# Two engines fetch the first batch ids of a four-layer LoRA kernel, and ACT issues the second batch's weights

## The reference, cut to what matters

```python
# x: (8, 128, 512) f32; itok_B_0_15: (8,) int32
def _L0_cond_ref(x, adapter_ids, weight):          # weight: (16, 512, 512)
    w = weight[adapter_ids]
    return jnp.einsum('bsi,boi->bso', x, w)
...
x = x + _L0_cond_ref(x, itok_B_0_15, L0_cond_weight)
x = x + _L1_cond_ref(x, itok_B_0_7, ...)   # dense 512x512 + 8 routed experts of rank 16
x = x + _L2_cond_ref(x, ..., itok_B_0_4)   # dense 512x512 + a LoRA of rank 32
x = x + _L3_cond_ref(x, ..., itok_B_2_6, 0)  # gated MLP 512-1376-512 + three LoRAs of rank 16
return x
```

## Time and profile before

| | |
|---|---|
| median of 3 runs | 298.38 us (298.31 to 298.52) |
| the profiled execution | 298.5 us, of which its span is 296.7 us |
| PE busy | 286.5 us, 97% of the span |
| DVE, ACT, POOL busy | 197.0, 143.8, 45.3 us |
| granted PE clock | 1.0 throughout |
| DMA in the first 35 us | from 4 us on the 16 DMA engines are busy 55% to 104% |

### The profile page before, as it was taken

The page is one execution under the profiler, slowest core; times in us unless marked ns, Lnnn a source line. Parts: engine busy times, 40 slices in busy tenths (PEclk is TensorE's granted clock), DMA queues, the critical chain, the costliest instruction groups (busy, mean ns, idle before and its releaser), DMA issues.

```text
span 296.7 us, 4572 instructions
## 1 busy us (share of the span) xinstructions
PE 286.5 (97%) x1624; PEld 235.8 (79%) x1624; DVE 197.0 (66%) x343; ACT 143.8 (48%) x255; POOL 45.3 (15%) x67
## 2 busy tenths in 40 slices
PE   5889999999999999999999999999999999999995
PEld 5358778888888788887788888888889888888884
DVE  1288897894656999897776776785747958342003
ACT  2378672513326279756646656566535783211000
POOL 1000000000804405243123213403000000000000
PEclk9999999999999999999999999999999999999999
DMA  5999974008504040300440520600193100022005
GB/s 165 342 393 395 343 243 108 0 0 248 178 0 101 0 145 0 121 23 0 124 159 4 167 115 16 197 3 26 48 354 126 56 0 0 0 73 71 0 2 141
DMA packets 23255, 33.29 MB, mean 112 GB/s; under 512 B 2624, under 2 KB 15424, under 8 KB 23104
## 3 DMA queue, kind: packets, MB, share of 16 engines
q1 hardware_dynamic: 22944, 32.47, 33.0%
q10 hardware_dynamic: 288, 0.52, 0.6%
HBM read 30.89 MB, written 2.10 MB: 111 GB/s over the span
## 4 chain that ended last, share of the span: by engine, by line
PE 86%; DVE 5%; DMA 4%; issue 2%; ACT 1%; SPq 1%; DVEq 0%; ACTq 0%
PE bank L1237 12%; PE bank L1238 12%; PE bank L1239 12%; PE bank L1360 10%; PE bank L1361 10%; PE bank L1362 10%; DMA w_raw<-in_w 4%; PE bank L1342 3%; PE bank L1192 2%; PE bank L1485 2%; PE bank L1221 1%; PE bank L1284 1%; PE bank L1174 1%; PE bank L1222 1%; PE bank L1223 1%
## 5 line engine op out<-in xcount | busy, mean ns | idle before, releaser
L546 ACT ACTIVATE part<-bank 128x512 f32<-128x512 f32 x44 | 26.1, 594 | 30.3 <-PE bank L1362 30.2
L1237 PE MATMUL bank<-act_hl,wd_hl 128*128 128x512 f32 (+1 forms) x99 | 36.5, 369 | 0.0
L1238 PE MATMUL bank<-act_hl,wd_hl 128*128 128x512 f32 (+1 forms) x99 | 36.3, 367 | 0.0
L1239 PE MATMUL bank<-act_hl,wd_hl 128*128 128x512 f32 (+1 forms) x99 | 36.2, 366 | 0.0
L1052 DVE TENSOR_TENSOR part<-bank,part 128x512 f32<-128x512 f32 x44 | 29.1, 682 | 6.7 <-PE bank L1342 6.6
L977 DVE SCALAR_TENSOR_TENSOR bgu_st<-bgu_st,lo_rows,bgu_raw 128x512 fp32r<-128x512 f32 x22 | 17.6, 836 | 11.6 <-ACT bgu_st L546 11.6
L803 DVE TENSOR_TENSOR w_hl<-w_raw,w_hl 128x512 fp32r<-128x512 f32 x29 | 19.0, 688 | 9.1 <-ACT w_hl L546 9.1
L546 ACT ACTIVATE act_hl<-act_f 128x512 fp32r<-128x512 f32 x22 | 13.6, 624 | 20.8 <-PE bank L1239 18.8
L803 DVE TENSOR_TENSOR act_hl<-act_f,act_hl 128x512 fp32r<-128x512 f32 x22 | 14.9, 691 | 12.9 <-ACT act_hl L546 12.8
L546 ACT ACTIVATE w_hl<-w_raw 128x512 fp32r<-128x512 f32 x29 | 17.7, 624 | 8.9 <-DMA w_raw<-in_w 8.6
L1239 PEld LDWEIGHTS bank<-act_hl,wd_hl 128*128 128x128 f32 x99 | 18.6, 188 | 3.1
(11 more groups left out here) (162 smaller groups left out, 695.1 us busy)
## 6 DMA issues: line engine op xcount, KB each, us to landing
w_raw<-in_w SPq DMA_DIRECT2D x22, 256.0 KB, 7.2
wgu_raw<-in_wgu SPq DMA_DIRECT2D x11, 512.0 KB, 4.1
bgu_raw<-in_bgu SPq DMA_DIRECT2D x40, 128.0 KB, 2.7
w_raw<-in_w SPq DMA_DIRECT2D x7, 512.0 KB, 7.6
wd_raw<-in_wd SPq DMA_DIRECT2D x4, 704.0 KB, 6.0
out<-x_f SPq DMA_DIRECT2D x7, 256.0 KB, 2.3
x_f<-in_xT SPq DMA_DIRECT2D x6, 256.0 KB, 8.4
w_raw<-in_w SPq DMA_DIRECT2D x1, 1024.0 KB, 4.9
```

Of the source, the lines that this page charges most:

```text
L546: return act.activation(dst, src, ACT.Copy)
L1237: pe.matmul(dst, w_hi, x[0][:, cols], start=start, stop=False)
L1238: pe.matmul(dst, w_hi, x[1][:, cols], start=False, stop=False)
L1239: return pe.matmul(dst, w_lo, x[0][:, cols], start=False, stop=stop)
```

## The change

SP fetches only id 0 ahead of c0 to c3. It fetches ids 2 to 7 behind c3's issue, in front of x_f of batch 2. ACT, after its two x_f transfers, fetches id 1 itself and issues the three pieces of batch 1. ids_of takes the stretch of ids and the engine as arguments, and the three issues have become the helper load_w0. The order of the waits and the buffers stay as they are.

```diff
+        def ids_of(src, last, first=0, end=B, engine=mybir.EngineType.SP):
+            _, ids = nc.values_load_multi_w_load_instructions(
+                src[0:1, first:end], engines=[engine], min_val=0, max_val=last,
...
+        W0_CUTS = ((0, 2), (2, 3), (3, 4))
+        def load_w0(queue, b, adapter):
+            for k, (first, end) in enumerate(W0_CUTS):
+                queue.dma_start(w0_raw[b % W0_RING][:, first:end],
+                                w0[adapter][:, first * D:end * D]).then_inc(w0_in[b % W0_RING][k], 16)
...
-            adapter0 = ids_of(ids0, w0.shape[0] - 1)
+            adapter0 = ids_of(ids0, w0.shape[0] - 1, 0, 1)
             for c in range(C):
                 sp.dma_start(w0_raw[0][:, c], w0[adapter0[0]][:, c * D:(c + 1) * D]).then_inc(w0c_in[c], 16)
-            for b in range(1, B):
-                adapter = adapter0[b]
-                if b >= 2:
-                    sp.dma_start(x_f[:, b], xT[b]).then_inc(x_in[b], 16)
+            adapter0 = [*adapter0, None, *ids_of(ids0, w0.shape[0] - 1, 2, B)]
+            for b in range(2, B):
+                sp.dma_start(x_f[:, b], xT[b]).then_inc(x_in[b], 16)
...
-                for k, (first, end) in enumerate(((0, 2), (2, 3), (3, 4))):
-                    sp.dma_start(w0_raw[b % W0_RING][:, first:end],
-                                 w0[adapter][:, first * D:end * D]).then_inc(w0_in[b % W0_RING][k], 16)
+                load_w0(sp, b, adapter0[b])
...
             for b in range(2):
                 act.dma_start(x_f[:, b], xT[b]).then_inc(x_in[b], 16)
+            load_w0(act, 1, ids_of(ids0, w0.shape[0] - 1, 1, 2, mybir.EngineType.Activation)[0])
```

More of the change, by code:

```diff
@@ L385, in bass_four_residual_layers @@
         block = ctx.enter_context(nc.Block())
+        def ids_of(src, last, first=0, end=B, engine=mybir.EngineType.SP):
+            _, ids = nc.values_load_multi_w_load_instructions(
+                src[0:1, first:end], engines=[engine], min_val=0, max_val=last,
+                skip_runtime_bounds_check_because="each id only forms the DRAM address of a transfer, "
+                                                  "and the transfer checks that address itself")
+            return ids
+        W0_CUTS = ((0, 2), (2, 3), (3, 4))
[3 more added lines that the diff above has]
+                                w0[adapter][:, first * D:end * D]).then_inc(w0_in[b % W0_RING][k], 16)
         @block.sync
         def _(sp):
[L390 to L396, removed]
-            adapter0 = ids_of(ids0, w0.shape[0] - 1)
+            adapter0 = ids_of(ids0, w0.shape[0] - 1, 0, 1)
             for c in range(C):
                 sp.dma_start(w0_raw[0][:, c], w0[adapter0[0]][:, c * D:(c + 1) * D]).then_inc(w0c_in[c], 16)
-            for b in range(1, B):
-                adapter = adapter0[b]
-                if b >= 2:
-                    sp.dma_start(x_f[:, b], xT[b]).then_inc(x_in[b], 16)
+            adapter0 = [*adapter0, None, *ids_of(ids0, w0.shape[0] - 1, 2, B)]
+            for b in range(2, B):
+                sp.dma_start(x_f[:, b], xT[b]).then_inc(x_in[b], 16)
                 if b == W0_RING:
```

## The result

The changed kernel is slower by 0.4%: 300.04 us in the median of 22 runs (298.81 to 302.57), beside 298.78 us for the kernel before in the same sessions (298.24 to 301.2). The ratio is 1.0039, with a 95% interval of 1.0021 to 1.0057. The forecast was 297.3 us. Three executions of those compared in this document took over 1000 us, two of the kernel before and one of e1_act_only; they are left out of the ratios.

What follows compares the result with a forecast made beforehand. Batch 3's L1221 at 21.58 us, held by the DMA queue and PE's work, sets the end. DMA side (0.4 + 0.7 = 1.1 us earlier) gives 20.5, PE side 20.4; the later gains 1.1: 297.3 us, range 296.4 to 298.5.

Steps and rivals of the forecast that it cites:

- Ids 2 to 7 behind c3: SP's second fetch, ahead of batch 2's x_f: about 2.1 us, x_f issued at 7.2, no cost while older transfers last.
- the four: The rivals: more is won (12%), single id not fetched faster (12%), batch 0 pays (22%), batch 0 pays more (10%).
- The sum: DMA side at the start: 0.4 + 0.7 = 1.1 us earlier, batch 3's first piece landing at 19.0, L1221 at 20.5.
- The PE side: c3 1.0 us later, batch 0 ending at 12.2, then 8.2 us of PE work: batch 3's L1221 at 20.4.
- the third rival: Batch 0 pays: c3 lands 1.6 to 2.2 us later, gain only 0 to 0.6, about 298.1 us; chance 22%.
- The fourth rival: Batch 0 pays more: c3 4.1 us later, batch 0 ends at 15.3, 1.9 us slower, 300.3 us; chance 10%.
- the first fetch: SP's load of id 0 alone takes 1.05 us instead of 1.48; c0 to c3 go out 0.4 us earlier.
- ACT's first issue: Batch 1's first issue, on ACT behind two register loads: at 3.8 us instead of 5.48 on SP.
- the share of 0.85 from 4 to 6.5 us: DMA share in this stretch at the start: forecast 0.7 or more, instead of 0.55; idle time filled worth 0.7 us.
- batch 1 without a wait for its weights: PE at batch 1's start: no wait before it, 0.29 us of waiting for a split gone.
- from batch 3's L1221 on everything moves along: Behind 21.58 us all hangs on PE, ACT and DVE progress, so the end shifts as much as L1221.

Runs made afterwards that it cites:

- e1_act_only: Changed kernel with SP fetching all eight ids first and no second fetch; ACT still fetches id 1 and issues batch 1: 0.9996 of the kernel before.
- e5: Changed kernel with SP's second fetch reading all eight ids from the first one on, not six from the third on: 1.0012 of the kernel before.
- e6: Changed kernel without ACT's part: SP issues batch 1 itself, and its second fetch, behind c3, reads all eight ids: 1.0024 of the kernel before.
- v8: Against the changed kernel: SP's second fetch reads eight ids behind batch 2's x_f; ACT fetches eight, issues batches 1 and 2; filler matmuls added: 0.9987 of before.
- e7_pause: Kernel before, with SP waiting for the end of batch 1's last transfer before issuing x_f of batch 2; no fetch moved: 304.24 us, one execution.
- e4: The changed kernel profiled once more, no edit, for the length of its second fetch: span 298.6 us.

## Why the prediction was wrong

*The step that failed* is the second one, "Ids 2 to 7 behind c3". It took the fetch at about 2.1 us, from the earlier trace rows, and wrote that it costs nothing, with a cover that is gone "only if the issue slips by 3 us". The fetch took 6.2 us in the profile, the issue of x_f slipped from the forecast 7.2 to 10.90, by 3.7, and the cover was gone. The bound held roughly: with the issue at 8.86 in e5 the engines stayed busy, with 10.90 they fell to a share of 0.62. The duration was wrong. The earlier trace rows held loads of one shape, eight ids from the first one, at the quiet start and at 31 and 34 us. No row had a load of another shape, or one beside the starting stream. Even for the same shape the upper end was too low: in other traces a load of eight ids at 33.7 us took 2.22 us (e6) and a pointer load at 30.4 us 2.45 (v8). That should have been an unknown price with a wide upper end, and it should have been a rival: none of the four had it.

*What the slip costs* was missing as well. I treated the queue as work at 324 GB/s or more that begins again where it stopped. In e7_pause some six microseconds at 240 to 266 GB/s follow the pause. As an estimate, six microseconds at 251 instead of 398 GB/s are a loss of 0.88 MB, 2.2 us at the full rate; in the changed kernel, 8 us at 298 are 0.80 MB, 2.0 us. The sum also left out that batch 3's first piece can't be issued before batch 0 ends: at the forecast's own 12.2 that is 1 us later than the 11.39 of before, where it counted 1.1 us earlier for its landing.

*The PE side* was mis-sized. c3 was taken 1.0 us later, with 2.1 as the upper bound. It landed at 4.3 + 7.9 = 12.2, 2.5 later, and batch 0 ended at 13.44. With the 8.2 us of PE work behind it this alone gives 21.6 for L1221 of batch 3: no gain, as the third rival had it, and the likelier course for ACT's half (e1: 0.9996). The other 0.8 us, up to 22.42, come from batch 3's late piece. The fourth rival named the right sign; in the profile of the result its cause is not the one, and its point of decision, batch 0's end at 13.4, was only just reached. In e4's execution its course came nearly to the number (batch 0's end at 15.50, it had 15.3; L1227 at 23.41, it had 23.5), but by a c1 that landed at 10.93 and a fall of the clock, which it didn't have. That its time, 300.3, is close to the measured 300.04 is luck in good part.

*Right were* the first fetch (0.83 us for one id, c0 issued at 2.65, 0.64 earlier; I had 0.4, at most 0.6; in e4 it was 0.02), ACT's first issue (3.81, I had 3.8), the share of 0.85 from 4 to 6.5 us, batch 1 without a wait for its weights, and that from batch 3's L1221 on everything moves along: 0.84 later there, 0.9 in the span. The rate in the filled stretch was 175 GB/s at that share of 0.85, though: I counted idle share as bytes won, and in a starting stream it isn't.

What stays open is why the loads take so long there. Shape and place both count, by the table. Whether an odd stretch is taken apart into several reads, and what a read waits for beside a starting stream, no run here shows. The same load of six ids took 4.41, 2.48 and 4.04 us in three executions, and nothing here says why. The Trainium skill, page "Runtime: NRT & Kernel Launch", section "Instruction fetch mechanics", gives some 200 ns for each register. At the quiet start one id took 0.58 to 0.85 us, three 1.8 and eight 1.5, which is no such line.

## What to carry to other kernels

A register load that stands between two DMA issues belongs to the transfer queue's path: price it at its worst, several microseconds beside running transfers, or put nothing urgent behind it. Keep a saturated queue from running empty: behind the pause of e7, 2.4 us of idle time from 12 to 15, the slow stretch cost about as much again by the estimate above, whatever makes it slow. A second issuing engine brought bytes forward here at the expense of the transfers beside them, so look at which of them the first consumer waits for. And take more than one trace of a kernel whose executions spread: the second one of the changed kernel lost its time in another place than the first.

## What the runs showed of the hardware

- A load of three registers from the first id on took longer than one of eight: 1.79 and 1.82 us in two traces against 1.47 to 1.51 in seven, at the same quiet place. One id took ACT 0.47 to 0.52 us behind a pointer load of 1.42, and SP 0.81 to 0.85 behind one of 0.86; where SP's pointer load took 1.74, its id took 0.58 (e4).
- After an empty queue (e7), DMA engines that were busy for 77% to 96% of the time moved 240 to 266 GB/s for six microseconds; in the stream of the kernel before they moved 398. In e5 they moved 295 GB/s for three microseconds at a share of 1.03, with no pause ahead.
- In e4 PE's granted clock fell from 1.0 to 0.5, 2.4 to 1.2 GHz, just behind a wait of 2.88 us, and the time at the lower level fell into the product that everybody waited for. In e1 it fell within a microsecond behind a wait of 1.92 us; in e7 it stayed at 1.0 behind one of 1.87.
